# Fewer signals per tile in a relational graph network with attention: two for a sum, one for a mask

## The reference, cut to what matters

```python
h = maximum(layernorm(x), 0)
for l in range(3):                                     # 8 edge types
    xr  = einsum('nd,rde->rne', h, W_rel[l])           # one table row per node and type
    agg = segment_sum(xr[edge_type, src], dst)         # gather 106250 rows, sum by target
    h   = relu(agg + h @ W_root[l] + bias[l])
x = x + h
h = maximum(layernorm(x), 0) @ Wv + bv
q, k = h @ wq + bq, h @ wk + bk
c = leaky(q[src] + k[dst], 0.2)
attn = exp(c - segment_max(c, dst)) / segment_sum(exp(...), dst)
out = x + segment_sum(h[src] * attn, dst)
```

## Time and profile before

| what | value |
|---|---|
| median of three timed executions | 5318.29 us (5300.09 to 5330.71) |
| profiled execution: its own time, its span | 5230.69 us, 5229.0 us |
| PE matmul, busy | 3608.1 us, 69% |
| POOL, busy | 3053.6 us, 58% |
| ACT, busy | 2196.4 us, 42% |
| DVE, busy | 1656.7 us, 32% |
| granted PE clock, mean | 0.82 |
| moved by DMA | 681.47 MB, 130 GB/s |

### The profile page before, as it was taken

The page is one execution under the profiler, slowest core; times in us unless marked ns, Lnnn a source line. Parts: engine busy times, 40 slices in busy tenths (PEclk is TensorE's granted clock), DMA queues, the critical chain, the costliest instruction groups (busy, mean ns, idle before and its releaser), DMA issues.

```text
span 5229.0 us, 56297 instructions
## 1 busy us (share of the span) xinstructions
PE 3608.1 (69%) x12674; PEld 2495.8 (48%) x12674; DVE 1656.7 (32%) x4423; ACT 2196.4 (42%) x6033; POOL 3053.6 (58%) x3302
## 2 busy tenths in 40 slices
PE   9986787777874877777775554544554666666667
PEld 4444554555552554545553343433433555545555
DVE  4533343333331222212221111111112545445444
ACT  2232443334442443433442333333333666556665
POOL 1145666666654666666664666666664566556664
PEclk9997888889887988888887677767766888888888
DMA  6553555555553444444443333333332333333332
GB/s 215 194 197 125 185 185 173 180 185 183 183 178 110 132 138 129 134 130 140 131 136 101 97 104 102 102 103 104 103 101 76 96 101 102 94 88 101 100 98 76
DMA packets 240051, 681.47 MB, mean 130 GB/s; under 512 B 60188, under 2 KB 111988, under 8 KB 215028
## 3 DMA queue, kind: packets, MB, share of 16 engines
q0 software_dynamic: 152400, 419.03, 27.6%
q10 hardware_dynamic: 57240, 186.43, 9.6%
q1 hardware_dynamic: 30092, 72.34, 3.8%
HBM read 501.99 MB, written 175.58 MB: 130 GB/s over the span
## 4 chain that ended last, share of the span: by engine, by line
PE 41%; another core or an unknown queue 26%; issue 14%; ACT 12%; DVE 6%; ACTq 1%; DVEq 0%; DMA 0%; SPq 0%
PE bank L1549 16%; PE sum_ps L1635 13%; PE sum_ps L1762 5%; ACT masks L1454 4%; ACT masks L1360 3%; PE bank L1718 2%; PE bank L1712 2%; DVE root L812 2%; PE turn_ps L1534 1%; ACT wide L1431 1%; ACT masks L1368 1%; PE sum_ps L1628 1%; ACT stage L1470 1%; ACT stage L1267 1%
## 5 line engine op out<-in xcount | busy, mean ns | idle before, releaser
L594 POOL DMA_INDIRECT ring<-table,code x2361 | 2236.4, 947 | 1377.8 <-issue 730.6
L1635 PE MATMUL sum_ps<-ring,masks 128*128 x5292 | 1445.6, 429 | 310.9 <-issue 295.6
L1635 PEld LDWEIGHTS sum_ps<-ring,masks 128*128 128x128 f32 x5292 | 1134.0, 218 | 587.6 <-issue 407.5
L1549 PE MATMUL bank<-wide,xT 128*128 128x512 f32 (+1 forms) x2744 | 1123.8, 563 | 4.1 <-issue 2.7
L594 POOL DMA_INDIRECT ring<-h_table,code x787 | 744.9, 946 | 503.1 <-SPq L734 254.8
L1360 ACT ACTIVATE masks<-node_row,local 128x128 f32<-128x128 f32 x2646 | 788.0, 387 | 24.8 <-issue 10.8
L1549 PEld LDWEIGHTS bank<-wide,xT 128*128 128x128 f32 x2744 | 514.3, 190 | 560.0 <-issue 548.7
L1762 PE MATMUL sum_ps<-ring,stage 128*128 x1764 | 541.7, 459 | 235.4 <-ACT stage L1470 151.2
L1258 ACT ACTIVATE xT<-turn_ps 128x256 f32<-128x256 f32 x196 | 75.5, 385 | 1441.8 <-remote 594.4
L1762 PEld LDWEIGHTS sum_ps<-ring,stage 128*128 128x128 f32 x1764 | 390.8, 235 | 314.6 <-issue 256.6
L1267 ACT COPY stage<-bank 128x512 f32<-128x512 f32 x441 | 244.3, 584 | 695.6 <-remote 429.2
(11 more groups left out here) (218 smaller groups left out, 2328.3 us busy)
## 6 DMA issues: line engine op xcount, KB each, us to landing
table<-stage ACTq DMA_DIRECT2D x96, 1024.0 KB
back<-table ACTq DMA_DIRECT2D x49, 1024.0 KB
table<-stage SPq DMA_DIRECT2D x48, 1024.0 KB
ring<-table,code POOLq DMA_INDIRECT x2361
ring<-h_table,code POOLq DMA_INDIRECT x787
h_table<-stage ACTq DMA_DIRECT2D x49, 130.0 KB
back<-h_table ACTq DMA_DIRECT2D x49, 130.0 KB
features<-xT SPq DMA_DIRECT2D x49, 128.0 KB, 4.0
```

The lines of the kernel that those rows point to most:

```text
L594: pool.indirect_dma_start(slot(c % RING, width), None, table, bass.IndirectOffsetOnAxis(ap=code[:, c:c + 1], axis=0)).then_inc(landed[n % ...
L1549: last = nc.tensor.matmul(bank[q][:, 0:width], xT[:, b, k, :], weights[:, k, 512 * q:512 * q + width], start=(k == 0), stop=(k == K - 1))
L1635: last = nc.tensor.matmul(sum_ps[b][:, 0:D], masks[:, b, s, :], at_offset(slots[s]), start=(s == 0 and l > 0), stop=(s == SLOTS - 1))
```

## The change

- `added` counts two signals per tile instead of five: PE signals after piece 2 and after piece 5, in all four passes. `need` is computed for two parts: a group that a tile last uses in its first 8 slots is released with piece 2, any later one with piece 5.
- The mask of a tile signals `mask_distance` once, after all 18 activations, and `mask_ready` once, after the last Relu. ACT has one wait between the two in place of five.
- In the third pass the second dot goes to another scratch tile, the two dots signal once and DVE waits once; the three small results signal once.
- POOL's preparation of `need` has three operations in place of ten.

```diff
+    PART_ENDS = (1, PIECES - 1)
+    PARTS = len(PART_ENDS)
+    SECOND_PART = (PART_ENDS[0] + 1) * GROUP
...
-            step(pool.tensor_tensor(need_part, need_sum, five.unsqueeze(1).to_broadcast(full_n), ALU.mult))
-            step(pool.tensor_tensor(need_sum, need_sum, need_part, ALU.add))
-            for k in range(1, PIECES):
-                step(pool.tensor_scalar(need_part, past, float(GROUP * k), None, ALU.is_ge))
-                if k < PIECES - 1:
-                    step(pool.tensor_tensor(need_sum, need_sum, need_part, ALU.add))
-                else:
-                    pool.tensor_tensor(need_sum, need_sum, need_part, ALU.add).then_inc(plan_marked, 1)
+            step(pool.tensor_tensor(need_sum, need_sum, parts_to.unsqueeze(1).to_broadcast(full_n), ALU.mult))
+            step(pool.tensor_scalar(past, past, float(SECOND_PART), None, ALU.is_ge))
+            pool.tensor_tensor(need_sum, need_sum, past, ALU.add).then_inc(plan_marked, 1)
...
-                for k, row in enumerate((wq_row, wk_row)):
-                    nc.vector.scalar_tensor_tensor(product[:, :], h_row[:, b, 0:D], 1.0, row[:, :], ALU.mult, ALU.mult,
-                                                   accum_out=denom[:, k:k + 1]).then_inc(dot_ready, 1)
-                    dve.wait_ge(dot_ready, 2 * i + k + 1)
+                for k, (row, to) in enumerate(((wq_row, product), (wk_row, summed))):
+                    last = nc.vector.scalar_tensor_tensor(to, h_row[:, b, 0:D], 1.0, row[:, :], ALU.mult, ALU.mult,
+                                                          accum_out=denom[:, k:k + 1])
+                last.then_inc(dot_ready, 1)
+                dve.wait_ge(dot_ready, i + 1)
...
-                    if s % GROUP == GROUP - 1 or s == SLOTS - 1:
-                        instruction.then_inc(mask_distance[b], 1)
+                instruction.then_inc(mask_distance[b], 1)
+                settle(act, l * USES[b] + j + 1)
+                act.wait_ge(mask_distance[b], l * USES[b] + j + 1)
                 for c in range(PIECES):
-                    settle(act, PIECES * (l * USES[b] + j) + c + 1)
-                    act.wait_ge(mask_distance[b], PIECES * (l * USES[b] + j) + c + 1)
                     part = masks[:, b, gathered(c)[0]:gathered(c)[-1] + 1, :]
-                    nc.scalar.activation(part, part, ACT.Relu, scale=-1.0, bias=1.0).then_inc(mask_ready[b], 1)
+                    instruction = nc.scalar.activation(part, part, ACT.Relu, scale=-1.0, bias=1.0)
+                instruction.then_inc(mask_ready[b], 1)
...
-                    pe.wait_ge(mask_ready[b], PIECES * use + c + 1)
+                    pe.wait_ge(mask_ready[b], use + 1)
...
-                    if added_by[c]:
-                        last.then_inc(added, added_by[c])
+                    if c in PART_ENDS:
+                        last.then_inc(added, 1)
...
-                last.then_inc(added, 1)
+                if c in PART_ENDS:
+                    last.then_inc(added, 1)
```

More of the change, by code:

```diff
@@ L210, in gnn_program @@
         piece_ends, piece_ends_i = (room(1, NT * PIECES, of).rearrange("p (t c) -> p t c", c=PIECES) for of in (F32, I32))
-        limit, five = room(HALF, 2), room(HALF, NT)
-        past, need_sum, need_part = (room(HALF, 2 * NT).rearrange("p (j t) -> p j t", t=NT) for _ in range(3))
+        limit, parts_to = room(HALF, 2), room(HALF, NT)
+        past, need_sum = (room(HALF, 2 * NT).rearrange("p (j t) -> p j t", t=NT) for _ in range(2))
         need_f = room(HALF, 2)
@@ L327, in columns, with tile_added @@
             return t[:, GROUP * P * c:min(GROUP * P * (c + 1), WIDTH)]
-        def pieces_done(l, tile):
-            return CREDIT + (l * NT + tile + 1) * PIECES
+        def tile_added(l, tile):
+            return CREDIT + (l * NT + tile + 1) * PARTS
         def bank_of_table(l, q):
@@ L728, in relay @@
                             _, counts = nc.values_load_multi_w_load_instructions(
-                                need[0:1, m:end], engines=[sp.engine], min_val=1, max_val=NT * PIECES,
-                                skip_runtime_bounds_check_because="counts of pieces, largest over the tiles")
-                        value = (counts[m % BATCH] & AT_MOST_PIECES) + (CREDIT + l * NT * PIECES)
+                                need[0:1, m:end], engines=[sp.engine], min_val=1, max_val=NT * PARTS,
+                                skip_runtime_bounds_check_because="counts of parts, largest over the tiles")
+                        value = (counts[m % BATCH] & AT_MOST_PARTS) + (CREDIT + l * NT * PARTS)
                         settle(sp, value)
@@ L1039, in sum_up @@
                     add_first_loops(i, j, b)
-                settle(dve, pieces_done(l, i))
-                dve.wait_ge(added, pieces_done(l, i))
+                settle(dve, tile_added(l, i))
+                dve.wait_ge(added, tile_added(l, i))
                 use = (l + 1) * USES[b] + j
@@ L1504, in attend @@
                         build_piece(i + 2, b, piece)
[L1506 to L1507 removed]
+            settle(act, tile_added(L - 1, NT - 1))
+            act.wait_ge(added, tile_added(L - 1, NT - 1))
             for c in range(PIECES):
@@ L1620, in at_offset, with sum_tile @@
                 return ring[:, bass.ds(offset, D)]
-            def sum_tile(l, where, j, b, pieces=range(PIECES), added_by=[1] * PIECES):
+            def sum_tile(l, where, j, b, pieces=range(PIECES)):
                 slots, groups = where
@@ L1658, in _ @@
                 turn_sum(l, 0, 0)
-                later = [0, 2] + [1] * (PIECES - 2)
                 for i in range(1, NT - 1):
@@ L1668, in _ @@
                         sum_tile(l, where, j, b, range(2, PIECES - 1))
-                        sum_tile(l, upcoming, PAIRS, 0, range(1), later)
+                        sum_tile(l, upcoming, PAIRS, 0, range(1))
                         sum_tile(l, where, j, b, range(PIECES - 1, PIECES))
@@ L1672, in _ @@
                     where = upcoming
-                sum_tile(l, where, PAIRS, 0, range(1, 2), later)
+                sum_tile(l, where, PAIRS, 0, range(1, 2))
                 next_table(l, NT - 2, PAIRS - 1, 1)
```

30 lines of the change are left out of this document (13 added, 17 removed).

## The result

Four executions of the changed kernel took 5213.8 to 5221.4 us (median 5218.3), four of the kernel before 5242.5 to 5330.7 us (median 5309.2). The ratio is 0.990, with an interval of 0.986 to 0.994. Ratios leave out executions over 1.5% above the fastest of their kernel, so that of 5330.7 us here (by the two medians it would be 0.983), and the ranges further on leave out four single executions of 6789 to 11697 us. The forecast of 5278 us was a ratio of 0.9924: the direction is right, and so is the size by the ratio. In us the median fell by 91, not by 40; 5218 us is inside the stated range, but outside the 5250 to 5292 us in which the likeliest case was to lie. How much of the reasoning is right is another matter: the experiments say that the gain did not come from where it was forecast.

What follows compares the result with a forecast made beforehand. POOL's gathers were taken as the bound, 988 us a pass plus halts for SP's release. Terms -35 - 5 + 0 = -40 us took the median 5318.3 to 5278 us; range 5190 to 5440.

Steps and rivals of the forecast that it cites:

- the likeliest case: Whole kernel: fewer halts of POOL, to lie in 5250 to 5292 us; chance 0.38.
- The third pass, -35 us: Third pass, sum's signals and release: 35 halts instead of 46, -35 us; bounds -70 and +147 us.
- POOL runs out after 8 gathers, 10.0 us, unless piece 2 is seen by then: Third pass: with two groups freed, POOL halts after 8 gathers if piece 2's signal is late; tile some 13 us.
- short and long tiles in turns: Third pass: tiles alternate between some 13 and some 30 us, two tiles having one halt and 43.4 us.
- The attention pass, -5 us: Attention pass release: fewer halts cancelled by later ones, -5 us; bounds -113 and +255 us.
- the rival of the later release: POOL runs out before piece 5 is executed; attention +67, relational +88, third pass -35, sum +120, 5438 us; chance 0.36.
- The first two passes, 0: First and second pass release: later groups against fewer halts, 0 us; bounds -110 and +265 us.
- PE's own time, 0: PE in all passes: three signals less per tile save 0 us, at best 20 us; the skill page's estimate 15 us.
- The stronger reading: PE's signals: if PE's stream is held up, few increments on the last matmul count for more than their price.
- Mask and dots, 0: Mask adds 29 us to ACT, beside PE's work, 0 us; two dots and three small results at most 2, taken as 0.
- POOL's preparation, 0: Before the first gather: seven small operations less, hidden by POOL's 39.58 us wait for the tables, 0 us.
- I carry the difference over: Whole kernel: the profiled execution's 87.6 us below the timed median is kept, turning 5190.7 into 5278 us.

Runs made afterwards that it cites:

- The kernel without late signals: The changed kernel, run on a third chip where PE's signals were not late; 4429 us, ratio 0.9998 to the kernel before.
- the first session: Changed kernel and each of its parts alone against the kernel before (median 5276 us); changed 0.9915, release alone 0.9906, mask alone 1.0013, dots alone 0.9999.
- the second session: Parts of the release changed singly, and new signal counts, against the kernel before (median 5229 us) on another chip; ratios 0.9974 to 1.0081.
- the two halves with two signals: Kernel before with two signals per tile's sum only in the attention pass (5268 us, 1.0060), and only in the relational passes (5232 us, 1.0004).
- the one with alternating tiles: Kernel before with PE signalling a tile's sum twice, in the three relational passes only; 5232 us, ratio 1.0004.
- chip B: The chip of the second session; there the kernel before took 5229 us at the median.
- The kernel with counts 1, 1, 0, 2, 1: Kernel before with relational counts 0, 2, 0, 0, 3 and attention counts 1, 1, 0, 2, 1 behind the five pieces; 5218 us, ratio 0.9974.
- the third session: Changed kernel and the kernel with counts 1, 1, 0, 2, 1 beside the kernel before, on a third chip; all 4429 us, both ratios 0.9998.

## Why the prediction was right, and where it wasn't

**The bound.** That POOL paces the kernel at 988 us for a pass, and that all over this are halts which come with late signals of PE, held: the kernel without late signals takes 985 to 996 us for a pass. Not every halt ends with a late signal: the first of an attention tile ends with PE's matmuls, though these halts too are gone where nothing is late. I took the lateness as something that the kernel does to itself by gathering. It isn't that alone; the same code on the same chip shows it in one session and not in another.

**The third pass, -35 us: too large by far.** It brought 4.2 us between the two profiles, 9 us between the means of two traces each in the first session, and nothing in the second. Two steps failed. The first is "POOL runs out after 8 gathers, 10.0 us, unless piece 2 is seen by then". In the changed kernel it was seen in most tiles, so POOL ran 16 gathers and made one halt, as before (54 waits for SP after, 46 before). The second is that short and long tiles in turns save a halt. Where they came in numbers, in the second session, three tiles kept their three halts and their 69.3 us.

**The attention pass, -5 us: this is where the gain was, and a term in its own right.** In the first session it is 1234 to 1236 us with two release points and 1259 to 1320 us with five: 23 to 86 us, against 9 us from the third pass. I had taken the 94 halts and their 2.4 us from one trace in which nearly all tiles are of the short kind. The bounds that I kept (-113 and +255) held both kinds. In the second session, where five points gave 1220 us, two cost 32 us more, where the rival of the later release had +67 us. Its mechanism isn't what the timeline shows, though. It had POOL run out before piece 5 is executed; in the tile of the changed kernel PE is through with piece 5 at 4239.84 + 0.59 = 4240.43, 3.8 us before the halt ends. By the whole attention pass of that trace, POOL ran out before PE was through with piece 5 in 3 of 47 tiles, and before piece 2 in 43; with two signals in the attention pass alone it is 17 and 43. So the late release is that of piece 2, in place of piece 1, and piece 5's only in part.

**The first two passes, 0.** In the first session (means of two traces each) 10 us less in the first pass, 4 us more in the second. In the second session the first pass is 1172.8, 1182.3 and 1193.1 us with two release points and 1182.5 us with five: the 10 us are within what traces differ by. Near 0, well inside the bounds.

**PE's own time, 0: not contradicted.** 36 matmuls take 9.55 us with two signals in them and 9.49 us with five. Over all third-pass tiles whose 36 matmuls run back to back the medians are 9.31 us (33 tiles) and 9.43 us (30 tiles), and single ones take 8.6 to 10.2 us in both traces. The estimate of 15 us from "TensorE: Matmul & The Clock Gate" of the Trainium skill is 0.08 us for a tile, too little to be told from 0 here. The stronger reading, that few signals count for more than their price, gets little from the kernel with five signals and two release points: its ratio is 1.0081, and that of the two halves with two signals 1.006 together, 9 us apart where over 15 us were expected, and their attention passes are alike.

**Mask and dots, 0: right**, at 1.0013 and 0.9999. ACT's idle time ahead of its Relus rose from 6.5 us to 34.1 us in all with the mask alone, 0.19 us for a mask, as forecast. In the profile of the changed kernel it is 85.6 us, not the 30 us that I gave as a sign; most of that, 68.9 us, is put down to "remote", and its cause stays open. It costs nothing: PE nowhere waits for a mask. The wait of 10.2 us is gone from its list. In DVE's groups the second dot has 0.0 us ahead of it in place of 1.7 us.

```profile
L1364 ACT ACTIVATE masks<-masks 128x512 f32<-128x512 f32 x588 | 321.6, 617 | 85.6 <-remote 68.9 <-ACT masks L1357 4.7 <-issue 1.2
```

**POOL's preparation, 0: right.** The first gather starts at 369.55 us, before at 368.28, and waits for the tables in both.

**From the profile to the median.** "I carry the difference over" was luck. The timed executions of the kernel before have no trace, but the mask alone, whose traced execution took 5327 us, has its excess in the attention pass (1320.0 against 1211.3 us). So the 87.6 us between the profiled and the timed executions are hardly an offset, but more long tiles in that pass, and the change acts on just that. The tiles of the third pass give a hint on which traces can be compared at all: 22.9 us is their median in the changed kernel's profile and in all four of the first session, 23.1 us in the profile of the kernel before and in three of the four of the second session (the fourth is the one with alternating tiles). The two profiles shown first may not be of one chip, and then the 4.2 us of the third pass aren't the change's either.

So the forecast came near -40 us by luck, with the wrong terms. In the first session some 9 us are from the third pass, and 23 to 86 us, by the trace compared with, from long attention tiles that the trace in hand hardly had. In the second session the sign was that of the later release, to which I had given 0.36. Over the four sessions the change is worth -0.9%, about +0.6% (put together from the two halves of its release; the changed kernel itself wasn't run in that session), 0.0% and 0.0%.

Four things stay open. The changed kernel itself was never run on chip B. The kernel with counts 1, 1, 0, 2, 1 never met a series of long tiles, so that the release of piece 3 makes them is shown by a timeline and by four tiles only. Why they were so frequent in the first session and rare in the second isn't known. And what makes PE's signals late is unknown: the longest waits for them end when POOL's gathers have drained, in each trace that has late ones, but whether the gap lets them through wasn't tested in that state, and traces with the same gathers do without any lateness.

## What to carry to other kernels

Finer signals aren't always better for a ring buffer: a release that lets the producer go on by one small step can push back the gap with which everybody else's signals come, by 5 us in the tile shown here; as a cause of all the long tiles this is argued, not shown. Nor are coarser ones always better: where long tiles were rare, two points cost 32 us in the same pass. Choose release points so that the producer either can go on for long or stops at once, and weigh each with a kernel that changes only the counts. Before terms are sized to 30 us from one trace, look at how far the executions of the kernel lie apart and where its passes differ between two traces; where a kernel swings by 100 us, a change may be worth nothing but that swing. And time it on more than one chip and more than once: here the same change is 0.9% faster, 0.6% slower or nothing.

## What was not expected of the hardware

The kernel before took 5276 us at the median in one session and 4434 us in another, on the same chip, both times with 15 or more executions within 2% of each other. The traces of the changed kernel in the two states (5220 us, and 4432 us in the third session) say where the time is. The engines are busy alike: PE 3531 and 3525 us, ACT 2204 and 2195 us, DVE 1648 and 1644 us, POOL 3050 and 3056 us. Of the 788 us between them 725 lie in the four passes, where POOL waits for SP 835 and 29 us. What differs is when PE's signals are seen while POOL gathers: 11.0 us between PE's end and DVE's start in the one state, 0.11 us in the other.

In the late state not all signals are held back alike. In the third pass of the changed kernel's first trace the next recorded update of `added` comes 2.3 us after PE's end of piece 2 and 10.8 us after that of piece 5, as medians over 45 and 46 tiles; in the kernel before it is 8.0 us behind piece 2. In the third session's trace it is 0.01 us for each of them. TensorE's mean granted clock was 0.82 in the late state and 0.89 without it, but with PE busy for the same time the clock explains none of the difference.
